# Recommender tower with one-hot look-ups: the id masks by a per-partition scalar in SBUF instead of a broadcast column in PSUM

## The reference

```
e = stack([tbl_0[ids[:, 0]], ..., tbl_25[ids[:, 25]]], axis=1)
combined = concatenate([dense[:, None, :], e], axis=1)          # 2048 x 27 x 128
interactions = einsum('bnd,bmd->bnm', combined, combined)
z = concatenate([dense, interactions[:, i < j]], axis=1)
h = concatenate([z, dense], axis=1)                              # 607 columns
h = maximum(h @ W_top1 + b_top1, 0); h = maximum(h @ W_top2 + b_top2, 0)
y = h @ W_top3
```

## Time and profile before

| | |
|---|---|
| time, median of 3 runs | 377.36 us |
| span of the profiled execution | 375.2 us |
| PE matmul busy | 329.8 us (88%) |
| POOL busy | 258.0 us (69%) |
| DVE busy | 198.1 us (53%) |
| ACT busy | 191.4 us (51%) |
| mean granted TensorE clock | 0.968 |

### The profile page before, as it was taken

The page is one execution under the profiler, slowest core; times in us unless marked ns, Lnnn a source line. Parts: engine busy times, 40 slices in busy tenths (PEclk is TensorE's granted clock), DMA queues, the critical chain, the costliest instruction groups (busy, mean ns, idle before and its releaser), DMA issues.

```text
span 375.2 us, 13452 instructions
## 1 busy us (share of the span) xinstructions
PE 329.8 (88%) x6048; PEld 297.8 (79%) x6048; DVE 198.1 (53%) x364; ACT 191.4 (51%) x234; POOL 258.0 (69%) x280
## 2 busy tenths in 40 slices
PE   0476856999989999999999999999899988999797
PEld 0475745998779978997799878997799867997586
DVE  3599741995049901993079704990099405940000
ACT  2587633456544655455444653465535563455323
POOL 6777777777777777777777777777777777774000
PEclk9998985999999999999999999999999999999969
DMA  6997492663236623662266324752266225423140
GB/s 158 258 260 183 119 317 55 140 207 90 51 91 148 199 52 76 141 211 63 61 141 198 92 59 96 191 145 59 70 149 196 73 54 127 112 56 71 35 67 2
DMA packets 55415, 45.72 MB, mean 122 GB/s; under 512 B 39444, under 2 KB 45179, under 8 KB 55359
## 3 DMA queue, kind: packets, MB, share of 16 engines
q1 hardware_dynamic: 45783, 26.91, 28.8%
q0 software_dynamic: 8704, 17.84, 18.0%
q10 hardware_dynamic: 871, 0.11, 0.2%
HBM read 37.91 MB, written 6.93 MB: 120 GB/s over the span
## 4 chain that ended last, share of the span: by engine, by line
PE 52%; POOL 25%; issue 12%; ACT 4%; DVE 3%; DMA 3%; ACTq 1%; SPq 0%; DVEq 0%
PE banks L441 27%; POOL rows L399 25%; PE banks L460 7%; PE mlp L479 6%; PE moved L424 5%; PE mlp L489 4%; PE mlp L520 2%; DVE masks L682 2%; DMA hot_ids<-in_ids_of_field_dram 1%; DMA rows<-in_tbl_dram,ids_sb 1%; ACT vectors L771 1%; DVE low L669 1%; ACT vectors L754 1%; PE banks L531 1%; PE mlp L500 1%
## 5 line engine op out<-in xcount | busy, mean ns | idle before, releaser
L399 POOL DMA_INDIRECT rows<-in_tbl_dram,ids_sb x272 | 257.1, 945 | 83.8 <-issue 81.1
L682 DVE TENSOR_TENSOR masks<-hot_ids,row_of 125x512 fp32r<-125x512 int32 (+1 forms) x336 | 181.5, 614 | 17.9 <-PE banks L441 13.4
L441 PE MATMUL banks<-masks,high 125*128 125x256 f32 x592 | 151.3, 295 | 18.9 <-DVE low L669 18.9
L441 PE MATMUL banks<-masks,low 125*128 125x256 f32 x592 | 146.9, 287 | 0.0
L441 PEld LDWEIGHTS banks<-masks,high 125*128 125x128 f32 x592 | 116.2, 196 | 20.9 <-issue 16.3
L441 PEld LDWEIGHTS banks<-masks,low 125*128 125x128 f32 x592 | 116.3, 196 | 0.1
L771 ACT ACTIVATE vectors<-moved 128x384 f32<-128x384 f32 (+1 forms) x80 | 87.8, 1097 | 3.9 <-PE moved L424 3.5
L754 ACT ACTIVATE vectors<-banks 128x512 f32<-128x512 f32 (+1 forms) x40 | 44.6, 1114 | 77.8 <-PE banks L441 77.8
L460 PEld LDWEIGHTS banks<-vectors 128*27 128x27 f32 x4096 | 45.6, 107 | 29.7 <-issue 23.1
L460 PE MATMUL banks<-vectors 128*27 128x27 f32 x4096 | 54.8, 196 | 14.5 <-issue 10.2
L691 DVE COPY vectors<-dense_sb 128x256 f32<-128x256 f32 x8 | 3.5, 435 | 103.1 <-PE banks L460 103.1
(11 more groups left out here) (33 smaller groups left out, 56.6 us busy)
## 6 DMA issues: line engine op xcount, KB each, us to landing
hot_ids<-in_ids_of_field_dram SPq DMA_DIRECT2D x32, 256.0 KB, 5.1
scratch<-products SPq DMA_DIRECT2D x28, 169.0 KB
rows<-in_tbl_dram,ids_sb POOLq DMA_INDIRECT x272
features<-scratch SPq DMA_DIRECT2D x7, 351.0 KB
w_sb<-in_tbl_dram SPq DMA_DIRECT2D x3, 448.0 KB
scratch<-products SPq DMA_DIRECT2D x28, 42.2 KB
dense_sb<-in_dense_dram SPq DMA_DIRECT2D x8, 128.0 KB, 4.8
hot_ids<-in_ids_of_field_dram SPq DMA_DIRECT2D x8, 128.0 KB
```

The costliest lines, as they stand in the source:

```text
L399: pool.indirect_dma_start(rows[:, (tile * TILE_ROWS + v) % RING, :], None, tables[f][:, :], bass.IndirectOffsetOnAxis(ap=ids_sb[:, tile, f ...
L441: last = nc.tensor.matmul(banks[:, j % BANKS, m * CHUNK:(m + 1) * CHUNK], part[:, part_of(j * PAIR + m, k), :], masks[:, mask % MASK_RING, ...
L682: nc.vector.tensor_tensor(masks[:, mask % MASK_RING, 0:size], hot_ids[0:PART_ROWS, n % ID_RING, 0:size], row_of[0:PART_ROWS, row:row + 1]. ...
```

## The change

The column moves from PSUM to SBUF, and the mask instruction becomes a tensor-scalar operation with one tensor input (the ids) and a pointer to one value per partition, in place of a tensor-tensor operation whose second input is that value repeated along the row. Sizes, counts, order, waits and results are the same.

```diff
-        row_of = ps("row_of", [128, BANK])
+        row_of = sb("row_of", [128, sum(KINDS)])
...
-                    nc.vector.tensor_tensor(masks[:, mask % MASK_RING, 0:size],
+                    nc.vector.tensor_scalar(masks[:, mask % MASK_RING, 0:size],
                                             hot_ids[0:PART_ROWS, n % ID_RING, 0:size],
-                                            row_of[0:PART_ROWS, row:row + 1].broadcast_to([PART_ROWS, size]),
+                                            row_of[0:PART_ROWS, row:row + 1], None,
                                             ALU.is_equal).then_inc(mask_made, 1)
...
-            nc.vector.tensor_copy(row_of[:, 0:sum(KINDS)], row_of_int[:, :]).then_inc(rows_numbered, 1)
+            nc.vector.tensor_copy(row_of[:, :], row_of_int[:, :]).then_inc(rows_numbered, 1)
```

## The result

The changed kernel takes 392.33 us (median of 4 runs, 389.95 to 394.33) against 377.53 us in the same session: a ratio of 1.039, with a 95% interval of 1.034 to 1.045. It is 14.8 us slower. The profiled execution's span grew from 375.2 to 391.2 us, by 16.0 us. The forecast was 397 us.

The account below looks back on a forecast made before the run. POOL's gathers were taken as the pacemaker, with PE close behind. The span 375.2 - 1.0 (saving) + 17.7 (hold) + 3 (gap) gave 394.9 us; with runs 2.2 us above the span, 397 us, range 376 to 424.

Parts of the forecast that it names:

- What bounds the kernel: POOL's gathers, one every 1.248 us, set the pace; each us lost before gather 246 reaches the end.
- The price of a mask: DVE masks drop from 677 to 410 ns (512 elements) and from 410 to 276 ns (256), two elements at a time.
- The doubt from the copies: fp32 copies inside SBUF took 426 and 391 ns for 256 elements, so masks might stay at 677 ns.
- The saving: DVE sheds 9.9 us of first-chunk mask work before `low`; 0 to 1.5 us reaches the end, 1.0 taken.
- The hold, 17.7 us: Masks on both DVE ports hold gathers arriving at random, 0.072 us each over 246 gathers: 17.7 us.
- gap term: Gathers caught in back-to-back masks wait for the run's end: 12 us in full, a quarter taken, 3 us.
- rival B: Gathers wait for whole runs of masks, or masks hold at today's length: 415 us, chance 0.23.
- A: The forecast itself, one mask holds one gather: 397 us, own range 388 to 411 us, chance 0.48.
- The term put at nothing: GpSimd's descriptor writing blocked in later parts of gathers: left out of the sum after six cases without effect.
- Rows 6 to 8: Gathers of 1.08 and 0.99 us beside a copy and an addition in SBUF; one of 0.94 beside another copy, not held.
- C: The two-port mode isn't entered: masks stay at 677 ns, nothing holds the gathers, 377 us; chance 0.14.
- D: Mode entered but POOL not held, gathers stay at 944 ns: 376.4 us, chance 0.10; faster variant to 372 us, 0.05.

Follow-up runs that it names:

- (3): 28 gathers left out of the kernel before and of the changed kernel: 373.47 us (ratio 0.991) and 371.65 us (ratio 0.988).
- (6): Kernel before plus trains of extra Vector instructions in seven DVE pauses, seven forms; then 20 tensor-scalar instructions of 512 in each pause: span 410.0 us.
- (5): Kernel before with the new form only for the first chunk's 42 masks: 380.01 us (1.006); only for the 80 masks of 256: 377.27 us (1.000).
- (4): Changed kernel with each 512-element mask made by two tensor-scalar instructions of 256: 377.65 us, ratio 1.001.
- (2): Kernel before with only the column moved to SBUF, tensor-tensor comparison kept: 384.89 us, ratio 1.022.

## Why the prediction was right, and which of its terms were not

*What bounds the kernel.* That POOL's delays before gather 246 arrive one for one held: 14.8 us of them, 15.0 us at the landing of that gather, 14.8 us in the median of the runs, and nothing that the times show once gathers were left out (3).

*The signs.* The mean gather came to 1.003 us (1.03 forecast), the last gather started at 357.4 us (364), PE's waits for rows were 15.3 us (over 15), and DVE's share was 42% (35%).

*The price of a mask.* The mode was entered. Some 480 ns for 512 elements (478 in the train of (6), 481 in the median of the changed kernel's large masks), against 410 forecast; the trains with half the size (341 ns in the median for 256) give 0.54 ns per element, half of the 1.04 of before, so two at a time as assumed, but a fixed part of 204 ns where I carried over 143 from the tensor-tensor rows. The doubt from the copies was empty: the copy without a stride took 734 ns in the mean for 1024 elements, where 1024 times 1.04 ns would be 1065. That the strides made the copies of rows 9 slow is likely, but no run takes a stride away from one of them.

*The saving.* I gave it 1.0 us and said that POOL would catch it. None of it can be seen at the end, and hardly any came as far as POOL: DVE shed 6 us of work ahead of the last `low`, not 9.9, and waited for ACT and the table loads instead (5). The last `low` ended at 42.7 us where it had ended at 42.6. In all DVE lost 35 us of busy time, not 79.

*The hold, 17.7 us.* The sum had 17.7 for the hold and 3 for the gap; the 14.8 us before gather 246 are 10.3 us of reads that waited for one mask, 1.2 us of waits for a second mask, and 3.3 us at the second place. So the hold as I meant it was sized 7 us too high, the gap term 2 us too high, and a term was missing. That the total came near the forecast is partly luck, since these errors, and those within the hold, offset each other in part. With 478 and 341 ns my own sum would have been 256 x 0.478^2 / 2 + 80 x 0.341^2 / 2 = 33.9 us^2 over 340 us, 24.5 us. But the hold isn't as long as the instruction. In the changed kernel 87 gathers read during a large mask. Of these, all 56 that read 248 ns or less before its end waited for that remainder (11 ns less at most) or longer, those at 335 to 346 ns were late by at most 121 ns, and those at 395 ns or more not at all but for one of 88 ns; these last delays arise at the second place and not at the read. Beside small masks nothing was late from 200 ns on (15 cases, 9 ns at most; the expectation in (4) counted 17). That fits a hold of about 267 and 133 ns, the time in which elements stream two at a time, and so does the difference of 133 ns between the places where held large and small masks end (1.19 and 1.06 us). Random arrivals at such short holds would cost only 256 x 0.267^2 / 2 + 80 x 0.133^2 / 2 = 9.8 us^2 over 340 us, 7.1 us. The other 3 us come because arrivals aren't random: a gather that makes a mask wait sets where the next masks end, and the reads bunch at 208 to 217 and at 234 to 248 ns before an end, inside the hold.

*The gap term, 3 us.* Its mechanism is real but rare: three reads waited for a second mask, 400 ns more each. That only these few did may be due to PE: it paces the masks, and DVE waited for it for 32.9 us in 32 places. The trains of (6), without that pacing, show waits of up to 6.9 us. I had named a gather of over 1.4 us as the sign of rival B; three gathers took 1.56 to 1.68 us, so the sign showed without B's price. The upper bound of A, 411 us, doesn't follow from its words either: 397 with the gap term in full, 12 us in place of 3, is 406 us.

*The term put at nothing.* I saw no effect of L704's copy on later parts of gathers in six cases and left the writing of descriptors out. The second place, 0.82 us after a gather's start, is such a later part and cost 3.3 us. Rows 9 had a trace of it: one copy of L704 took 450 ns in place of some 390, one of L691 492 in place of 426, and they end 1.06 and 1.20 us after a gather's start, where held masks end. That this place is the writing of descriptors is not shown; what is shown is that the masks with two tensor inputs, as in (2), neither wait nor hold there, and the new form does both.

*Rows 6 to 8.* The two held gathers weren't chance. In (6) additions and copies hold gathers as well. With the copy of L691 that held none the read came 69 ns before its end; no run here tells why it let the gather pass.

*The rivals.* C fell with the masks' 478 ns, D with the gathers' 1003 ns mean, B with the time, 392 us against its 415. The Trainium skill (SBUF — State Buffer, Who interferes with whom) has the one that comes second blocked until the other is through, for the whole instruction. The runs agree on who contends and disagree on the length: the first 200 ns of a mask held no gather (4), and a gather too holds a mask in parts of its time only, not for all of its 944 ns.

The Trainium skill's two fp32 elements a cycle for a tensor-scalar in SBUF (VectorE: DVE Perf Modes, The perf-mode tier table) agree with 0.54 ns per element here, against 1.04 in the form of before.

## What to carry to other kernels

A Vector instruction with one tensor input, from SBUF to SBUF in 4-byte elements, is quick, but it and POOL's indirect DMAs hold each other up; where POOL paces the kernel, as here, a comparison with a broadcast column in PSUM is the better mask, though it takes 40% longer. Before making an engine off the path faster, look whether its rows stretch another engine's: the maximum beside the median, and what ran beside each long one, show it in the trace before. Look at the other engine's outliers as well: a contention shows on whichever side came second. If the quick form is wanted, cut it to 256 elements (here DVE is then as busy as in the kernel before), or see that DVE waits between them, and never run large ones back to back beside gathers.

## What the runs showed that I had not expected

- A train of 20 tensor-scalar instructions of 512 elements kept one gather waiting for 2.3 to 6.9 us, in seven trains of seven.
- Gathers and masks hold each other. A gather holds masks near its end, up to some 0.925 us after its start, and by that sets where the next masks end; so trains fall in step with the gathers of 1.25 us. In step they cost 0 ns a gather (256 elements, or two inputs), 75 ns (1024) or 350 ns (512, column in PSUM); the size of the instruction alone predicts none of them.
- A gather can be held twice, at its read and some 0.82 us after its start. A mask with two inputs in SBUF holds it at the read alone.
- Halving each instruction, at 39 us more of DVE work, took the loss from 14.8 us to nothing that can be measured. POOL's waits became DVE's: 27.8 us in 140 masks.
- The hold falls into the last 267 or 133 ns of an instruction of 478 or 341 ns, as the trace times it.
